# A graph kernel's destination pass with two records to a partition and 512-byte dense runs

## The reference

```python
h = jnp.maximum(_layernorm(x, axis=-1), 0.0)
x = x + _L0_gnn_ref(h, edge_index, edge_attr_32, ...)   # by src: sum, max and mean of edge attributes,
                                                        # then relu(f @ W1 + b1) @ W2 + b2
h = jnp.maximum(_layernorm(x, axis=-1), 0.0)
agg = jax.ops.segment_sum(h[src], dst, num_segments=100000)
x = x + jax.nn.relu(agg @ W.T + b)
```

## Time and profile before

| | us |
|---|---|
| median of 3 timed runs | 1623.49 |
| lowest and highest | 1609.49, 1625.28 |
| span of the profiled execution | 1619.7 |
| busy: PE, DVE, ACT, POOL | 880.8, 995.8, 552.6, 848.1 |

### The profile page before, as it was taken

How to read it: one execution, slowest core, us unless ns; L and a number is a source line. 1 busy time by engine, 2 the same in 40 slices (tenths; PEclk the granted TensorE clock), 3 DMA queues, 4 the chain that set the end, 5 groups by cost and what they waited for, 6 DMA issues and landing times.

```text
span 1619.7 us, 28924 instructions
## 1 busy us (share of the span) xinstructions
PE 880.8 (54%) x8466; PEld 635.9 (39%) x8466; DVE 995.8 (61%) x2746; ACT 552.6 (34%) x1726; POOL 848.1 (52%) x863
## 2 busy tenths in 40 slices
PE   0120145787888788888795113545455445455553
PEld 0010022555555555565574102433334333333442
DVE  9899944677777777778795113444455444444553
ACT  0300123444444444444451213333344333333430
POOL 4733175566656666666610755555566555555400
PEclk9985556899989989889998555555555555555555
DMA  1000012688777877777797114787688767887889
GB/s 42 0 0 0 15 39 57 159 224 225 206 199 201 218 211 209 206 205 214 215 256 225 27 31 100 180 203 176 161 184 195 174 165 178 201 189 180 190 204 205
DMA packets 486483, 253.92 MB, mean 157 GB/s; under 512 B 417657, under 2 KB 449373, under 8 KB 486323
## 3 DMA queue, kind: packets, MB, share of 16 engines
q1 hardware_dynamic: 376066, 157.65, 39.3%
q10 hardware_dynamic: 85168, 75.08, 15.4%
q0 software_dynamic: 25088, 19.32, 7.0%
HBM read 159.45 MB, written 92.43 MB: 156 GB/s over the span
## 4 chain that ended last, share of the span: by engine, by line
ACT 20%; ACTq 19%; another core or an unknown queue 18%; issue 16%; DVE 15%; PE 9%; DMA 2%; SPq 1%; POOL 1%; DVEq 0%; POOLq 0%
ACTq L680 10%; ACT hn L759 6%; ACT xa L665 4%; ACTq L712 3%; ACTq L686 3%; ACT rec L706 3%; ACT hid L693 2%; ACTq L673 2%; DVE ka L976 2%; DVE kb L976 2%; ACT rec L700 2%; DVE ka L977 2%; DVE kb L977 1%; PE p_m L1428 1%
## 5 line engine op out<-in xcount | busy, mean ns | idle before, releaser
L589 POOL DMA_INDIRECT xa<-node_table,gi x392 | 370.7, 946 | 340.8 <-ACT hn L759 142.5
L577 POOL DMA_INDIRECT xa<-in_edge_attr_dram,gi x392 | 402.0, 1026 | 266.7 <-issue 94.9
L759 ACT ACTIVATE hn<-xa,nmr,rstd 128x64 f32<-128x64 f32 x392 | 140.4, 428 | 340.9 <-issue 292.0
L1228 DVE RECIPROCAL rstd<-sd 128x4 f32<-128x4 f32 x98 | 17.5, 178 | 303.9 <-ACT sd L751 210.5
L700 ACT CAST rec<-p_m 128x256 bf16<-128x256 f32 x164 | 60.7, 370 | 292.7 <-remote 259.6
L1480 PE MATMUL p_g<-ident,hn 128*128 128x128 f32 x196 | 64.9, 431 | 156.1 <-ACT hn L759 94.8
L1125 DVE TENSOR_TENSOR_SCAN feats<-c_rows,feats,p_g 64x512 f32<-64x512 f32 x97 | 122.9, 1267 | 16.4 <-PE p_g L1412 8.2
L693 ACT ACTIVATE hid<-p_z,bias_z 128x512 f32<-128x512 f32 x98 | 113.1, 1154 | 53.9 <-issue 23.2
L1428 PE MATMUL p_m<-w_s,hid 128*128 128x64 f32 x784 | 121.2, 300 | 6.6 <-issue 6.5
L1127 DVE TENSOR_TENSOR_SCAN feats<-c_rows,feats,p_g 32x512 f32<-32x512 f32 x97 | 123.3, 1271 | 1.4
L1420 PE MATMUL p_z<-feats,w_s 96*128 96x512 f32 x196 | 119.5, 695 | 3.4 <-DVE feats L1127 2.6
(11 more groups left out here) (277 smaller groups left out, 1820.1 us busy)
## 6 DMA issues: line engine op xcount, KB each, us to landing
records<-rec ACTq DMA_DIRECT2D x196, 196.0 KB
win<-records SPq DMA_DIRECT2D x392, 85.8 KB
node_table<-dout SPq DMA_DIRECT2D x49, 512.0 KB
din<-node_table SPq DMA_DIRECT2D x49, 512.0 KB
out_dram<-dout SPq DMA_DIRECT2D x49, 512.0 KB
din<-in_x_dram SPq DMA_DIRECT2D x48, 512.0 KB
c_rows<-rows_src ACTq DMA_DIRECT2D x141, 128.0 KB
win<-records SPq DMA_DIRECT2D x392, 42.9 KB
```

The costliest lines, as they stand in the source:

```text
L577: g.indirect_dma_start(out=xa[n % XRING][:, t, 0:FE], out_offset=None, in_=edge_attr, in_offset=bass.IndirectOffsetOnAxis(ap=gi[0][:, BT * ...
L589: g.indirect_dma_start(out=xa[k % XRING][:, t, :], out_offset=None, in_=T, in_offset=bass.IndirectOffsetOnAxis(ap=gi[1][:, BT * n + t:BT * ...
L759: last = s.activation(hn[n % 2][:, t, :], xa[k % XRING][:, t, :], ACT.Relu, bias=nmr[n % 2][:, t:t + 1], scale=rstd[n % 2][:, t:t + 1])
```

## The change

Only the destination pass and its preparation are changed.

- A window now covers two groups (256 nodes): 192 records (2 x `PAIR`) from the start of the even group, records 2p and 2p+1 on partition p of 96. SP loads four of them for a step, with 784 bytes in a run. `upper_windows` on ACT is gone. The start of every second group suffices, so `start_row[1]` holds half as many, and the test for exceptions asks for at most 192 edges in two groups instead of 112 in one.
- A load brings records that may belong to any of the 256 nodes. The one-hot matrices are now compared with `odd_even`, which holds the 128 even nodes and then the 128 odd ones. So each of the 8 record columns has two matrices (`oneh` of shape `PER`, 2, `UNIT`), and a PSUM column block s is the sum over both record columns of its pair: 2 x 3 matmuls for each s, 48 for a step.
- With even and odd nodes in separate column blocks, partition p holds nodes 2p and 2p+1 of a pair of groups, so the dense rows move in runs of 512 bytes.
- `base_i`, `node_i16` and `sign_out` share one tile.

```diff
@@ -30,6 +30,7 @@
+PAIR = 96
@@ -188,7 +190,7 @@
-        oneh = [[sb(f"oneh{s}_{b_}", [P, *shape, UNIT], BF16) for b_ in range(HRING)] for s, shape in enumerate(((PER // 2, 3), (PER,)))]
+        oneh = [[sb(f"oneh{s}_{b_}", [P, *shape, UNIT], BF16) for b_ in range(HRING)] for s, shape in enumerate(((PER // 2, 3), (PER, 2)))]
@@ -296,7 +298,7 @@
-            return sum(16 * PER // (2 if j < BLOCKS else 1) for j in range(k % WRING, k + 1, WRING))
+            return 16 * PER // 2 * (k // WRING + 1)
@@ -309,7 +311,7 @@
-            return at.rearrange("(s p) d -> p s d", p=P)
+            return at.rearrange("(q p a) d -> p q (a d)", p=P, a=2)
@@ -320,7 +322,7 @@
-            return tile[:, :, :].rearrange("p b (s d) -> p (b s) d", d=D)
+            return tile[:, :, :].rearrange("p b (q r) -> p (b q) r", r=2 * D)
@@ -376,7 +378,7 @@
             def windows(side, m):
 
                 g = BLOCKS * side + m
-                starts = start_row[side][0:1, PER * m:PER * (m + 1) if side == 0 else PER * m + PER // 2]
+                starts = start_row[side][0:1, PER * m:PER * (m + 1)] if side == 0 else start_row[side][0:1, PER // 2 * m:PER // 2 * (m + 1)]
                 _, at = nc.values_load_multi_w_load_instructions(starts, engines=[mybir.EngineType.SP], min_val=0, max_val=E,
                                                                  skip_runtime_bounds_check_because="each start is a count of rows, lowered to its limit on the chip")
                 for n in range(AHEAD + 1) if m == 0 else [min(m + AHEAD, BLOCKS - 1)]:
@@ -389,7 +391,8 @@
-                        sp.dma_start(win[g % WRING][0:WP, q, :], recs[side][bass.ds(at[q], WP), :]).then_inc(win_in[g % WRING], 16)
+                        sp.dma_start(win[g % WRING][0:PAIR, 2 * q:2 * q + 2, :],
+                                     recs[side][bass.ds(at[q], 2 * PAIR), :].rearrange("(p a) r -> p a r", a=2)).then_inc(win_in[g % WRING], 16)
@@ -511,6 +514,8 @@
+            link(g.iota(node_i16[:, :], [[1, 2], [2, UNIT]], base=0, channel_multiplier=0))
+            link(g.tensor_copy(odd_even[:, :], node_i16[:, :]))
@@ -552,18 +557,20 @@
-            link(g.tensor_copy(start_row[1][:, :], over[:, :]))
+            link(g.tensor_copy(start_row[1][:, 0:GROUPS // 2], over[:, 0:GROUPS:2]))
-            link(g.tensor_tensor(over[:, 0:LAST], start_f[:, 1:LAST + 1], start_f[:, 0:LAST], ALU.subtract))
-            link(g.tensor_scalar(over[:, 0:LAST], over[:, 0:LAST], float(WP), None, ALU.is_gt))
-            g.tensor_tensor(over[:, 0:LAST], over[:, 0:LAST], over2[:, 0:LAST], ALU.add).then_inc(s_rows1, 1)
+            link(g.tensor_tensor(over[:, 0:LAST // 2], start_f[:, 2:LAST + 1:2], start_f[:, 0:LAST:2], ALU.subtract))
+            link(g.tensor_scalar(over[:, 0:LAST // 2], over[:, 0:LAST // 2], float(2 * PAIR), None, ALU.is_gt))
+            g.tensor_tensor(over[:, 0:LAST // 2], over[:, 0:LAST // 2], over2[:, 0:LAST:2], ALU.add).then_inc(s_rows1, 1)
-                link(g.tensor_copy(t[96:P, :, :], mask[1][96:P, 0:1].unsqueeze(2).to_broadcast([P - 96, PER, UNIT])))
+                link(g.memset(t[96:P, :, :, :], 0.0))
+                link(g.tensor_copy(t[96:P, 0:PER:2, :, :].rearrange("p s h n -> p s (h n)"),
+                                   mask[1][96:P, 0:1].unsqueeze(2).to_broadcast([P - 96, PER // 2, 2 * UNIT])))
@@ -665,19 +672,6 @@
-
-            def upper_windows(m):
-
-                g = BLOCKS + m
-                starts = start_row[1][0:1, PER * m + PER // 2:PER * (m + 1)]
-                _, at = nc.values_load_multi_w_load_instructions(starts, engines=[mybir.EngineType.Activation], min_val=0, max_val=E,
-                                                                 skip_runtime_bounds_check_because="each start is a count of rows, lowered to its limit on the chip")
-                for n in range(AHEAD + 1) if m == 0 else [min(m + AHEAD, BLOCKS - 1)]:
-                    stored = BLOCKS + n
-                    act.wait_ge(rec_out[stored % RRING], 16 * (stored // RRING + 1))
-                act.wait_ge(expanded, g - WRING + 1)
-                for q in range(PER // 2):
-                    s.dma_start(win[g % WRING][0:WP, PER // 2 + q, :], recs[1][bass.ds(at[q], WP), :]).then_inc(win_in[g % WRING], 16)
@@ -768,7 +762,7 @@
-                for n in range(BLOCKS + DST_WIN):
+                for n in range(BLOCKS + DST_REC):
@@ -781,8 +775,6 @@
-                    if valid(n - DST_WIN):
-                        upper_windows(n - DST_WIN)
@@ -1140,13 +1132,10 @@
-                if side == 1:
-                    v.tensor_tensor(rel[k % 2][0:WP, :, :], win[k % WRING][0:WP, :, KEY].unsqueeze(2).to_broadcast([WP, PER, 2]),
-                                    base_f[0:WP, PER * m:PER * (m + 1)].unsqueeze(2).to_broadcast([WP, PER, 2]), ALU.subtract).then_inc(rel_ok, 1)
-                    return
-                v.tensor_tensor(rel[k % 2][0:WP, :, :].rearrange("p (q a) i -> p q a i", a=2),
-                                win[k % WRING][0:WP, :, KEY].rearrange("p (q a) -> p q a", a=2).unsqueeze(3).to_broadcast([WP, PER // 2, 2, 2]),
-                                base_f[0:WP, PER * m:PER * (m + 1):2].unsqueeze(2).unsqueeze(3).to_broadcast([WP, PER // 2, 2, 2]),
+                rows = WP if side == 0 else PAIR
+                v.tensor_tensor(rel[k % 2][0:rows, :, :].rearrange("p (q a) i -> p q a i", a=2),
+                                win[k % WRING][0:rows, :, KEY].rearrange("p (q a) -> p q a", a=2).unsqueeze(3).to_broadcast([rows, PER // 2, 2, 2]),
+                                base_f[0:rows, PER * m:PER * (m + 1):2].unsqueeze(2).unsqueeze(3).to_broadcast([rows, PER // 2, 2, 2]),
@@ -1157,9 +1146,10 @@
-                    v.tensor_tensor(hot[0:WP, :, :].rearrange("p s (n i) -> p s n i", i=2),
-                                    nodes[:, 0:UNIT // 2, :].unsqueeze(1).to_broadcast([WP, PER, UNIT // 2, 2]),
-                                    rel[k % 2][0:WP, :, :].unsqueeze(2).to_broadcast([WP, PER, UNIT // 2, 2]), ALU.is_equal).then_inc(hot_ok, 1)
+                    turns = odd_even[0:PAIR, :].rearrange("p (n i) -> p n i", i=2)
+                    v.tensor_tensor(hot[0:PAIR, :, :, :].rearrange("p s h (n i) -> p s (h n) i", i=2),
+                                    turns.unsqueeze(1).to_broadcast([PAIR, PER, UNIT, 2]),
+                                    rel[k % 2][0:PAIR, :, :].unsqueeze(2).to_broadcast([PAIR, PER, UNIT, 2]), ALU.is_equal).then_inc(hot_ok, 1)
@@ -1439,9 +1429,11 @@
                 pe.wait_ge(hot_ok, k + 1)
                 if side == 1:
                     for s in range(PER):
-                        for w in range(3):
-                            last = mm(to[:, D * s:D * (s + 1)], oneh[1][m % HRING][:, s, :], win_words[k % WRING][:, s, D * w:D * (w + 1)],
-                                      start=w == 0, stop=w == 2)
+                        for a in range(2):
+                            slot = s // 2 * 2 + a
+                            for w in range(3):
+                                last = mm(to[:, D * s:D * (s + 1)], oneh[1][m % HRING][:, slot, s % 2, :], win_words[k % WRING][:, slot, D * w:D * (w + 1)],
+                                          start=a == 0 and w == 0, stop=a == 1 and w == 2)
                     last.then_inc(expanded, 1)
                     return
                 for q in range(PER // 2):
```

More of the change, by code:

```diff
@@ L170, in build @@
         above = sb("above", [P, SPAN, GROUPS], F16)
-        sign_out = sb("sign_out", [P, COLS])
         over = sb("over", [1, GROUPS])
@@ L927, in beside_turn @@
                     dve.wait_ge(s_rows1, 1)
-                    v.reduce_sum(wrong[0:1, 1:2], over[:, 0:LAST], AX.X)
+                    v.reduce_sum(wrong[0:1, 1:2], over[:, 0:LAST // 2], AX.X)
                     v.tensor_scalar(wrong[0:1, 5:6], start_f[:, LAST:LAST + 1], float(E), None, ALU.not_equal)
```

6 lines of the change are left out of this document (4 added, 2 removed).

## The result

| | before | after |
|---|---|---|
| median of 4 timed runs, us | 1621.88 | 1644.57 |
| lowest and highest | 1609.49, 1625.28 | 1640.17, 1652.96 |
| ratio | | 1.0185, interval 1.0119 to 1.0251 |
| span of the profiled execution | 1619.7 | 1645.6 |

The forecast was 1507 us.

The account below looks back on a forecast made before the run. It took ACT's sequencer to bound the destination pass. Blocks falling from 6.63 to 5.4 us gave -109 us over 89 blocks and the drain -7, so 1619.7 + 3.8 - 116, stated as 1507 us; range 1460 to 1590.

Parts of the forecast that it names:

- the term for PE's unexplained stalls: Destination pass, "issue" idle before the expanding matmuls: 0.33 to 1.65 us a block, taken as 0.9.
- the prediction's own sum for PE: Destination pass, PE's matmuls, transposes and hand-offs: 4.45 us a block without stalls, 5.35 with them.
- ACT bounds the pass: Destination pass: ACT's sequencer sets the block, with window issues taking 2.7 to 4.7 us of each.
- POOL's floor of 5.00 us: Destination pass: four unchanged gathers a block, 1.25 us apart, set the least new block length.
- Block of 5.4 us: Destination pass: new block length, set by the slowest engines, POOL at 5.00 and PE at 5.35 us.
- The block of 6.63: Destination pass before the change: block length read from 89 blocks between 981.1 and 1569.9 us.
- One-hots: DVE in the destination pass: 2048 elements a partition take 1.21 us against 0.68, +0.53 us.
- Drain: Last 50 us, paced by SP's windows: -9 us over 11 blocks, +2 for the last block, so -7.
- PE's free burst of 48: Destination pass: 48 expanding matmuls without stalls take 2.52 us at the lower clock.
- rival 3: Destination pass: TensorE's clock rises, POOL bounds at 5.05 us a block, total 1473 us; chance 0.15.
- The sign given for the DMA share: Destination pass of the changed profile: dense packets halved and DMA share not above 0.8.
- Rival 1: Destination pass: twice the matmuls meet twice the stalls, PE 7.75 us a block, total 1720 us; chance 0.13.

Follow-up runs that it names:

- e4: Changed kernel with the destination pass's four gathers a block replaced by plain POOL DMAs of consecutive rows: 1322.2 us, ratio 0.8106.
- e3: Kernel before with windows in four loads of 2 x 112 records on SP, none on ACT: 1632.14 us, ratio 0.9997.
- e14: Repeat of e3 (kernel before, windows on SP only) on a third chip of the first kind: 1631.5 us, ratio 0.9982.
- e1: Kernel before with every burst of 24 expansion matmuls in the destination pass issued twice: 1684.29 us, ratio 1.0299.
- e15: Repeat of e1 (kernel before, bursts issued twice) on a third chip of the first kind: 1687.99 us, ratio 1.0293.
- e7: Changed kernel with two of a block's four destination-pass gathers by index, the other two plain DMAs: 1342.87 us, ratio 0.8234.
- e6: Changed kernel with each destination-pass gather by index fetching rows 0 to 127: 1662.19 us, ratio 1.0186.
- e8: Changed kernel with a 128 x 128 POOL memset after each destination-pass gather, on the first kind of chip: 1611.65 us, ratio 0.986.
- e18: e3 again (kernel before, windows on SP only) on a chip of the second kind: 1330.58 us, ratio 0.9607.
- e5: Kernel before with the destination pass's gathers by index replaced by plain POOL DMAs of the same size: 1486.92 us, ratio 0.9103.
- e17: Changed kernel itself beside the kernel before, on a chip of the second kind: 1334.49 us, ratio 0.9631.
- e13: Changed kernel itself beside the kernel before, on a third chip of the first kind: 1659.83 us, ratio 1.0131.
- e2: Changed kernel with only the first record column multiplied, 24 matmuls in a burst: 1617.15 us, ratio 0.991.
- e11: Kernel before with a 128 x 128 POOL memset after each destination-pass gather, second kind of chip: 1405.85 us, ratio 1.0179.

## Why the prediction was wrong

**The step that failed** is the term for PE's unexplained stalls. The prediction placed it between 0.33 and 1.65 us a block and took 0.9; it measured 2.77 in the recorded run, where the prediction's own sum for PE gives 4.45 + 2.77 = 7.22 us against a block of 7.14 over the same 400 us. The reason given for 0.9 was that the source pass "differs by having no window issues on ACT and fewer small packets". Both differences were then given to the destination pass (packets fell from 152461 on q1 to 83012 over the same 400 us) and the stalls grew. With e4 they vanished. The stall comes with gathers by index close together, and only on some chips.

The wrong term hid a wrong picture. All of the sum treats the engines as independent but for semaphores: POOL's gathers were a floor of 5.00 us and otherwise harmless. On this kind of chip, POOL gathering without pause slows everyone else until the eight `xa` slots are full; then POOL stands (111.3 us in 400 for `hn`) and the others catch up. A block costs what that alternation costs. A freed ACT brought nothing (e3, e14) and more matmuls cost time directly (e1, e15). That the alternation works in just this way, and explains these two, is argued from the order of time; what the runs show is that the crawling needs gathers by index close together (e4, e7), not scattered addresses (e6), and a small gain from a pause (e8).

Point by point:

- *ACT bounds the pass, 2.67 to 4.7 us of each block.* Right on the second kind of chip: e18 moves these issues to SP and gains 3.9%. Right also on the first kind once nothing crawls (5.61 us a block in e5). With the crawling it is worth 0.0 to 0.2% (e3, e14). The chain was read rightly, but it named whichever engine was late at the end of a crawl as well as the one that bounds.
- *POOL's floor of 5.00 us.* It is the bound in e17, though nearer 5.2: 215.06 / 214 = 1.005 us a gather there, not 0.95, since some take 1.2 to 1.6. With 0.30 between them that is 5.22.
- *Block of 5.4 us.* 5.32 in e17, so the number came true there, by POOL's gathers and not by PE at 5.35; 7.20 in the recorded run. The block of 6.63 from which the prediction counted down (588.8 / 89 is in fact 6.62) is about a microsecond longer than e5's 5.61, and the change does not take away the gathers by index that make it longer. Even in e17 the gain is 51 us, not 116. If all of it is in the destination pass, the kernel before had 5.32 + 51 / 97 = 5.84 us a block there, not 6.95.
- *One-hots.* 1.21 us predicted; the page of the changed kernel has 1.218 (the row below). Right.
- *Drain.* -7 us predicted. From the last `hn` to the end of the span it took 49.8 us before and 51.1 after, +1.3, so the gain given to SP's windows does not show.
- *PE's free burst of 48.* 2.52 predicted, 2.61 measured at the lower clock in the recorded run and 2.71 in e17; 1.64 predicted for the upper clock (rival 3), 1.60 measured.
- *DMA and clock.* The sign given for the DMA share, not above 0.8, held: 0.60, and 0.79 in e17. The clock rose to 0.66, and to 0.77 in e17, so rival 3's mechanism came in half. On the second kind of chip neither moved the time: e18, with bursts of 24 and the dense runs of the kernel before, has a clock of 0.60 and a DMA share of 1.01 from 1000 to 1280 us (the row below) and takes 1330.58 us against e17's 1334.49. On the first kind no run parts them from the rest.
- *Rival 1, stalls by instruction.* It comes nearest: stalls of 1.65 / 24 = 69 ns a matmul before and 2.77 / 48 = 58 ns after, past the 2.2 us from which it was to decide, and the kernel is slower. Its price of 1720 us was too high for two reasons: it took twice 1.65 where 2.77 was measured, which alone makes 7.75 us 7.22, and it set this against 6.63, where the whole pass had 6.95 us a block before and 7.20 after. It had 0.13 because the source pass, with 36 matmuls a block, stalled less before these. But that pass has its unnamed waits elsewhere: the waits of the kernel before, 400 to 800 us, have ACT idle for 173.6 us with no engine named (e17 has no such row), and on the second kind of chip the pass ends 124 us earlier (`hn` begins at 771.8 in e17, at 896.3 in the recorded run). That its gathers cause them is likely, but no run on the first kind took them away.

The row of e18's stage, 1000 to 1280 us:

```profile
1000.00:1280.00 280.00, 145.63 (x1672) 126.73 (x1673) 176.33 (x810) 145.55 (x494) 206.12 (x208) 0.60 1.01 235
```

The row of the one-hots, from the page after:

```profile
L1150 DVE TENSOR_TENSOR oneh<-odd_even,rel 96x2048 bf16<-96x2048 bf16 x98 | 119.4, 1218 | 185.3 <-remote 164.6
```

and that wait of ACT in the source pass, kernel before:

```profile
ACT rec L700 <- remote: 173.6, 55, 6.8
```

- *The halves add up roughly.* On the first kind: windows off ACT -0.2% (e14), 24 more matmuls +2.9% (e15), so +2.7%; the change measured +1.3% there (e13) and without its extra matmuls -0.9% (e2). Some 0.7 to 1.4% is left for the halved dense packets and the higher clock; no run isolates it.

The Trainium skill, DMA: Bandwidth & Descriptors, section "Issuing engines are not separate DMA queues", was the rule that the prediction went against: issuing from several engines saves only the sequencer's time, which is usually small. The runs agree with it on one kind of chip (0.9997 and 0.9982). On the other, what is saved is again the sequencer's time, but it was worth 3.9% of the kernel (0.9607), which is not small.

**Still open.** What sets the two kinds apart isn't known. Each of the six chips showed one kind in all its runs of the kernel before (7 to 19 a chip), but nothing shows whether it is the chip itself or something else that ran beside it. Nor is it shown what the crawling streams wait for. The trace names no semaphore; scattered addresses (e6) and the amount of data (e4 moves as much) are ruled out; POOL's own load is too (e7). How far apart gathers by index must be is open.

## What to carry to other kernels

The chain by engine, over the whole span, from the page of the kernel before that the prediction had:

```profile
ACT 20%; ACTq 19%; another core or an unknown queue 18%; issue 16%; DVE 15%; PE 9%; DMA 2%; SPq 1%; POOL 1%; DVEq 0%; POOLq 0%
```

Idle time that the profile puts down to "issue" or to another core in a one-core program, on several engines at once, is a cause of its own: before pricing a change, look at what runs in exactly those stretches, and at the longest of a group of register instructions (a `MOVE` of 29 ns with a maximum near 700). "issue" alone is no such sign: e17's chain has 20.7% of it, much of it POOL's 0.30 us between gathers, and nothing crawls. A share of the chain is worth its face value only if nothing else would fill it; a run that removes only that share (e3, e18) tells. Where gathers by index close together are the cause, a plain load between them (e7) or a short pause (e8, -1.4%) is the lever, and on a chip without the effect the same pause costs (e11, +1.8%).

## What was not expected of the hardware

- Gathers by index issued by POOL 1.25 us apart stretch the other engines' instruction streams to steps of about 0.7 us on three of six chips; the same bytes by plain DMAs from POOL do not (a `MOVE` of up to 727 ns against at most 37, each in a stretch of 240 or 280 us). The kernel before takes 1632 to 1634 us on those chips and 1383 to 1385 on the others.
- It costs more than any part of the change: about 1.9 us of a block's 7.20 by the estimate above, where the whole change is worth +1.3 to +1.9% of the time or -3.7%.
- TensorE's granted clock in the destination pass rose from 0.51 to 0.66 when its bursts doubled in the recorded run. On the second kind of chip it is 0.60 with bursts of 24 (e18) and 0.77 with bursts of 48 (e17), at nearly the same time, with POOL's gathers on the chain in both.
